# Window attention of a fused two-layer kernel: units of two images (128 query rows by 64 keys), the last four queries of each image in a path of their own

## What is computed

```python
# 16 heads of width 16, per image of S = 68 tokens
q, k, v = (x @ Wq + bq), (x @ Wk + bk), (x @ Wv + bv)      # split into 16 heads
scores = einsum('bhqd,bhkd->bhqk', q, k) / sqrt(16)
allowed = (j <= i) & (i - j < 64)                          # causal, a window of 64 keys
attn = softmax(where(allowed, scores, -1e30))
out = einsum('bhqk,bhkd->bhqd', attn, v) ... @ Wo + bo
```

## Time and profile before

| | |
|---|---|
| median of 3 runs | 1057.34 us (1054.91 to 1061.70) |
| the profiled execution: its time | 1059.86 us |
| the profiled execution: its span, first to last instruction | 1058.1 us |
| mean granted TensorE clock over the span | 0.965 |
| the attention stage, from its first to the first instruction of the next | 52.5 to 225.3 us, 172.8 us |
| TensorE busy in it | 170.6 us |
| DVE / ACT / POOL busy in it | 143.5 / 117.7 / 98.6 us |

### The profile page before, as it was taken

How to read it: one execution, slowest core, us unless ns; L and a number is a source line. 1 busy time by engine, 2 the same in 40 slices (tenths; PEclk the granted TensorE clock), 3 DMA queues, 4 the chain that set the end, 5 groups by cost and what they waited for, 6 DMA issues and landing times. The chain is left out here.

```text
span 1058.1 us, 29663 instructions
## 1 busy us (share of the span) xinstructions
PE 947.0 (90%) x10380; PEld 745.1 (70%) x10398; DVE 589.4 (56%) x1463; ACT 413.5 (39%) x1102; POOL 520.6 (49%) x714
## 2 busy tenths in 40 slices
PE   8899999988747999999999998789888957999996
PEld 6667777777634888888888876355556635888895
DVE  1778888865994777433333325676887551111111
ACT  2267677734243344444443422222333222333431
POOL 0055665610604777777777627777772002433432
PEclk9999999999969999999999999887999987999998
DMA  7010000002004888877788723344483056476650
GB/s 256 1 46 2 0 0 0 1 12 75 1 1 161 292 283 261 272 247 224 242 265 253 230 89 100 100 113 122 122 289 80 21 191 218 143 262 222 266 155 25
DMA packets 79820, 149.28 MB, mean 141 GB/s; under 512 B 18892, under 2 KB 53327, under 8 KB 75760
## 3 DMA queue, kind: packets, MB, share of 16 engines
q1 hardware_dynamic: 34768, 77.15, 21.7%
q0 software_dynamic: 17712, 47.88, 16.0%
q10 hardware_dynamic: 27248, 23.09, 6.5%
HBM read 200.22 MB, written 31.73 MB: 219 GB/s over the span
## 5 line engine op out<-in xcount | busy, mean ns | idle before, releaser
L1332 POOL DMA_INDIRECT x_x<-m_x_rows,x_idx x170 | 165.7, 975 | 75.1 <-issue 35.6
L1358 PE MATMUL x_pup<-x_xt,x_w 128*128 128x128 f32 (+1 forms) x2176 | 182.9, 250 | 0.0
L1358 PEld LDWEIGHTS x_pup<-x_xt,x_w 128*128 128x128 f32 (+1 forms) x2176 | 166.9, 165 | 5.9 <-issue 5.7
L1623 POOL DMA_INDIRECT rl_y<-m_y_rows,rl_idx x136 | 134.2, 986 | 43.6 <-issue 36.3
L1439 DVE TENSOR_TENSOR x_hid<-x_gate,x_pup 128x128 f32<-128x128 f32 x170 | 48.9, 288 | 148.3 <-ACT x_gate L1411 140.9
L1372 PE MATMUL x_pdown<-x_w,x_hid 128*128 128x256 f32 (+1 forms) x408 | 104.2, 389 | 0.3 <-DVE x_y L1446 0.3
L1407 ACT ACTIVATE x_xt<-x_pturn 128x256 f32<-128x256 f32 x170 | 65.3, 384 | 89.3 <-PE x_pturn L1343 86.2
L442 POOL TENSOR_TENSOR wa_probs<-wa_probs,wa_peak 68x544 f32<-68x544 f32 x64 | 69.9, 1092 | 57.6 <-DVE wa_peak L593 54.9
L2420 DVE TENSOR_TENSOR x_y<-x_pdown,x_b 128x256 f32<-128x256 f32 x21 | 8.9, 425 | 151.7 <-PE x_pdown L2374 151.7
L2406 ACT ACTIVATE x_hid<-x_pup,x_b 128x128 f32<-128x128 f32 (+1 forms) x200 | 52.8, 357 | 95.9 <-PE x_pup L2357 95.8
L1411 ACT ACTIVATE x_gate<-x_pup 128x128 f32<-128x128 f32 x170 | 47.2, 278 | 92.4 <-PE x_pup L1358 91.7
(11 more groups left out here) (344 smaller groups left out, 1904.7 us busy)
## 6 DMA issues: line engine op xcount, KB each, us to landing
x_w<-in_experts SPq DMA_DIRECT2D x204, 384.0 KB
late_w<-in_w SPq DMA_DIRECT2D x28, 1024.0 KB
m_y_rows<-x_y ACTq DMA_DIRECT2D x170, 128.0 KB
xT<-in_w SPq DMA_DIRECT2D x12, 1024.0 KB, 6.0
xn<-in_w SPq DMA_DIRECT2D x10, 1024.0 KB, 10.3
h<-in_w SPq DMA_DIRECT2D x10, 1024.0 KB, 14.0
m_x_rows<-xn SPq DMA_DIRECT2D x34, 128.0 KB, 1.8
x_x<-m_x_rows,x_idx POOLq DMA_INDIRECT x170
```

Of the source, the lines that this page charges most:

```text
L1332: nc.gpsimd.indirect_dma_start(x[:, s, :], None, x_rows, bass.IndirectOffsetOnAxis(ap=idx[:, s:s + 1], axis=0))\
L1358: mm = nc.tensor.matmul(pup[rows:rows + wide, bank, m * P + side * wide:m * P + (side + 1) * wide], w[:, lane, first:first + wide], xt[:, ...
L1623: nc.gpsimd.indirect_dma_start(y[:, t % YR, kk, :], None, y_rows, bass.IndirectOffsetOnAxis(ap=idx[:, n:n + 1], axis=0))\
```

## The change

A unit becomes two images by one half: the first 64 queries of both images are the 128 partitions, the first 64 keys of 8 heads the 512 columns. There are 32 units (16 pairs of images by two halves, c changing fastest), unit u = step; all is written out, with no loop. A block of 4 images is four steps. Row sums are now a reduction on DVE (`add_up`) of the exponentials, followed by a reciprocal of 8 columns per row, and POOL multiplies the probabilities by it (`normalise`) before they are transposed; the matmuls by ones are gone. Transposes take two heads at once (128x128, eight per unit). The values are stored for both images' 64 tokens with the two heads of a pair block-diagonal (`vals`, two heads times 64 keys = 128 rows by 32 columns), so a weighing is 16 matmuls of 128 rows, 32 output partitions and 64 columns.

The last four queries (which see 68 keys) go a way of their own, once per pair of images: 2 images x 16 heads x 4 queries = 128 rows by 68 keys. In it DVE has seven more kinds of instruction (`last_spread`, `last_mask`, `last_peak`, `last_shift`, `last_invert`, `last_normalise`, `last_pick`), TensorE four (scores, `last_turn`, `last_weigh`, `last_sum`) and ACT three (`last_exp`, `last_move`, `last_place`). The values of the last four tokens of four images are a job of their own (`vt`, `vtail`).

The core of the diff (constants, buffers, waits and the old bodies are left out; the old bodies stand above):

```diff
@@ tensor
+                def score(unit):
...
+                    for i in range(2):
                         for g in range(STRIPS):
                             strip = slice(g * STRIP, (g + 1) * STRIP)
+                            mm = nc.tensor.matmul(pscore[i * HALF:(i + 1) * HALF, g, 0:P], queries[strip, i, :],
+                                                  kheads[strip, unit % 2, i, :, :].rearrange("p m n -> p (m n)"),
                                                   start=True, stop=True)
+                    if c == 0:
...
+                        for i in range(2):
+                            for cc in range(DC):
...
+                                mm = nc.tensor.matmul(pl_score[at:at + LROWS, :],
+                                                      lq[:, pair % 2, cc, i, :, :].rearrange("p h q -> p (h q)"), keys[:, i, :],
+                                                      start=True, stop=True)
+                    mm.then_inc(scored, 1)
...
+                    for n in range(2):
+                        first = blk * CB + (2 * int(kind[1]) + n) * S
+                        for kc in range(DC):
+                            for odd in range(2):
+                                mm = nc.tensor.matmul(pjob[odd * HALF:(odd + 1) * HALF, n * P:(n + 1) * P],
+                                                      xT[:, kc, first:first + HALF], wv[:, kc, odd * P:(odd + 1) * P],
+                                                      start=(kc == 0), stop=(kc == DC - 1))
...
+                def last_turn(pair):
+                    pe.wait_ge(l_ready, pair + 1)
...
+                    nc.tensor.transpose(pl_main, lmain[:, :, :].rearrange("p o n -> p (o n)"), ident)
+                    nc.tensor.transpose(pl_tail, ltail[:, :, :].rearrange("p n q -> p (n q)"), ident).then_inc(l_turned, 1)
+
+                def last_weigh(pair):
+                    slot, first = pair // 2 % 2, pair % 2 * 2
+                    pe.wait_ge(l_moved, pair + 1)
+                    pe.wait_ge(jobs_moved, done_by(2 * pair, "vt"))
+                    for i in range(2):
+                        for c in range(DC):
+                            at = (i * DC + c) * LROWS
+                            nc.tensor.matmul(pl_out[at:at + LROWS, :], lmainT[:, at:at + LROWS],
+                                             vals[:, slot, first + i, c * (HC // 2):(c + 1) * (HC // 2), :]
+                                             .rearrange("p t n -> p (t n)"), start=True, stop=False)
+                            mm = nc.tensor.matmul(pl_out[at:at + LROWS, :], ltailT[:, at:at + LROWS],
+                                                  vtail[:, slot, c * P:(c + 1) * P], start=False, stop=True)
+                    mm.then_inc(l_weighted, 1)
+
+                def last_sum(pair):
+                    pe.wait_ge(l_picked, pair + 1)
+                    nc.tensor.matmul(pl_sum, lout[:, :, :].rearrange("p h n -> p (h n)"), const("row_sel"),
+                                     start=True, stop=True).then_inc(l_summed, 1)
+
+                pe.wait_ge(w_in, 96)
+                for (blk, kind), into in zip(FIRST, (pout, pjob, pturn, plast)):
+                    project(wq if kind[0] == "q" else wk, int(kind[1]), blk, into)
+                for step in range(STEPS + 3):
+                    jobs = jobs_of(step)
+                    if step < STEPS:
+                        score(step)
+                    if step >= 3:
+                        weigh(step - 3)
+                    if step >= 3 and step % 2 == 1:
+                        last_weigh((step - 3) // 2)
+                    for job in jobs[:1]:
+                        do_job(*job)
+                    if step >= STEPS:
+                        keep_running(3)
+                    if 0 <= step - 2 < STEPS:
+                        turn(step - 2)
+                    for job in jobs[1:]:
+                        do_job(*job)
+                    if 2 <= step < STEPS + 2 and step % 2 == 0:
+                        last_turn(step // 2 - 1)
+                    if step >= 3 and step % 2 == 1:
+                        last_sum((step - 3) // 2)
+                keep_running(3)
@@ gpsimd
+                nc.gpsimd.memset(vals[:, :, :, :, :], 0.0).then_inc(vals_set, 1)
...
+                spread(0)
+                for step in range(STEPS + 1):
+                    if step + 1 < STEPS:
+                        spread(step + 1)
+                    if step < STEPS:
+                        shift(step)
+                    if step >= 1:
+                        normalise(step - 1)
@@ vector
+                for step in range(STEPS + 3):
+                    even = step % 2 == 0
+                    if step < STEPS:
+                        mask(step)
+                        if even:
+                            last_mask(step // 2)
+                        find_peak(step)
+                        if even:
+                            last_peak(step // 2)
+                            last_shift(step // 2)
+                    if 1 <= step <= STEPS:
+                        add_up(step - 1)
+                        invert(step - 1)
+                    if even and 2 <= step <= STEPS:
+                        last_invert(step // 2 - 1)
+                        last_normalise(step // 2 - 1)
+                    if not even and (step + 1) // 2 < NPAIR:
+                        last_spread((step + 1) // 2)
+                    if not even and step >= 3:
+                        last_pick((step - 3) // 2)
@@ scalar
+                    if even and step >= 4:
+                        last_place((step - 4) // 2)
+                    if 0 <= step - 3 < STEPS:
+                        place(step - 3)
+                    if 1 <= step <= STEPS:
+                        exp(step - 1)
+                    if not even and step <= STEPS:
+                        last_exp((step - 1) // 2)
+                    for job in jobs[:1]:
+                        move_job(*job)
+                    if 0 <= step - 2 < STEPS:
+                        move_turned(step - 2)
+                    for job in jobs[1:]:
+                        move_job(*job)
+                    if even and 2 <= step < STEPS + 2:
+                        last_move(step // 2 - 1)
```

More of the change, by code:

```diff
@@ L529, in body @@
[L529 to L539 removed]
+                        nc.tensor.matmul(pjob[:, 0:D], wq[:, 0, 0:P], wq[:, 1, :], start=True, stop=True)
@@ L554, in body @@
-                        if not (start and step < 3):
-                            v = (step - 3) % UNITS
-                            weigh(unit - 3, (step - 3) % 2, v % ABLK, v // ABLK, start and step == 3)
-                blocks(pe, body)
-                n_units = NBLK * UNITS
-                for step in range(3):
-                    keep_running(pjob, 2)
-                    if step < 2:
-                        turn(n_units + step - 2, (step - 2) % 4, step % 2, False)
-                    v = (step - 3) % UNITS
-                    weigh(n_units + step - 3, (step - 3) % 2, v % ABLK, v // ABLK, False)
@@ new lines, in score, with turn @@
+                    mm.then_inc(scored, 1)
+                def turn(unit):
+                    pe.wait_ge(normalised, unit + 1)
+                    if unit:
+                        pe.wait_ge(turn_moved, unit)
+                    for two in range(HC // 2):
+                        mm = nc.tensor.transpose(pturn[:, two * P:(two + 1) * P],
+                                                 probs[:, unit % 4, 2 * two:2 * two + 2, :].rearrange("p h n -> p (h n)"), ident)
+                    mm.then_inc(turned, 1)
@@ new lines, in _ @@
+                act.wait_ge(w_in, 96)
+                for (blk, kind), src in zip(FIRST, (pout, pjob, pturn, plast)):
+                    move_job(blk, kind, src)
+                for step in range(STEPS + 4):
+                    even = step % 2 == 0
+                    jobs = jobs_of(step)
+                    if even and step >= 4:
[14 more added lines that the diff above has]
+                        last_move(step // 2 - 1)
```

486 lines of the change are left out of this document (256 added, 230 removed).

## The result

The changed kernel takes 1148.65 us (median of 3 runs, 1141.46 to 1152.25), against 1057.34 us before: ratio 1.0824, 95% interval 1.0769 to 1.088. It is 91 us slower. The forecast was 1069 and its range ended at 1083. The profiled execution took 1152.25 us.

A forecast was written before the change was run, and what follows sets the result against it. TensorE was taken to bound the attention stage. Its step terms summed to 16 W - 30.0, +11.6 us at W = 2.6, so 1057.3 + 11.6 = 1069 us; range 1034 to 1083, likeliest case 1056 to 1078.

The forecast's parts named there:

- The wait at `last_turn`: In even steps TensorE waits about 0.1 us for `l_ready` from DVE's chain, making the step 4.7 us.
- TensorE's list as the bound: The attention stage is as long as TensorE's work; DVE, ACT and POOL stay below TensorE's 4.5 us per step.
- The granted clock stays 1.00: In the attention stage the clock stays at 1.00, as TensorE stays busy.
- W: Time of one `last_weigh` on TensorE in odd steps: between 0.46 and 3.0 us, taken as 2.6; no change at 1.9.
- that the term of 0.90: Time of a unit's transposes on TensorE: 8 x 0.11, 0.90 us with what surrounds them.
- that of 0.65: Time of a unit's weighing on TensorE: 32 records in 0.61 us, 0.65 with one more change of array shape.
- 17.1 + 2 W: Length in us of a block of four steps in attention, against 20.3 for the same four images before.
- Cheap `last_weigh`: Rival: `last_weigh` takes 0.46 to 1.2 us, giving 1040 or 1035 us; chance 0.33 with or without the DVE hold.
- Halves in sequence: Rival: array halves do not overlap, scores 0.78 and value jobs 1.85 us, +20 on the forecast, 1089; chance 0.10.
- Fewer elementwise instructions, no time: Rival included in the forecast: DVE, ACT and POOL fall to about 100, 95 and 92 us without gain; no separate chance.
- DVE's chain sets steps: Rival: DVE holds steps at 3.4 us and `last_turn`'s wait at 4.5, gain ending near 1030; within cheap `last_weigh`'s 0.33.
- four signs of being wrong: `last_weigh` below 1.9 us, value jobs near 1.9, TensorE waiting for ACT's moves between jobs, or a stage outside attention moving.

The follow-up runs named there:

- e2: The changed kernel without the last four queries' path, their result columns filled by a copy of the input: 1004.81 us, ratio 0.9486.
- e5: The changed kernel with the last queries' spreading, shift, masking and normalising moved or folded so VectorE's work avoids GpSimd's way: 1058.74 us, ratio 1.0015.
- e8: The changed kernel with four unused matmuls run before `last_turn` in even steps, in place of TensorE's wait: 1099.07 us, ratio 1.0358.
- e4: The changed kernel with the last queries' later stages one step later and `last_weigh`'s 128-row matmuls grouped before its 16-row ones: 1078.22 us, ratio 1.0179.
- e3: The changed kernel with `last_turn`, `last_move`, `last_weigh`, `last_pick`, `last_sum` and `last_place` each one step later: 1083.85 us, ratio 1.0232.
- e7: The kernel before, with 16 unused groups of matmuls of `last_weigh`'s shapes and order added to its q/k jobs: 1106.76 us, ratio 1.043.
- e6: e5 with `last_weigh`'s four 128-row matmuls put first, then its four 16-row ones: 1033.69 us, ratio 0.9742.
- e11: The kernel before, with one unused 68x68 VectorE multiplication reading PSUM added ahead of each reciprocal: 1057.49 us.
- e9: e6 with `last_turn` and `last_sum` moved ahead of the step's second job: 1032.46 us, ratio 0.9731.

## Why the prediction was wrong

**The wait at `last_turn`, and with it TensorE's list as the bound: wrong.** The step that failed is the sentence that DVE's chain in an even step is "some 4.4 in all", so that `last_turn` "waits about 0.1". The chain from the mask to `l_ready` measured 145.53 - 140.49 = 5.04 us, where the forecast's own terms from the mask on (4.4 less 0.91 before it) make 3.5. TensorE came to `last_turn` 143.70 - 139.37 = 4.33 us after the step's scores, which is the 4.29 of the forecast (by chance: its terms were too long and part of the step ran at half clock). The small instructions were priced "0.15 to 0.33 each", from rows of other kinds: the earlier trace rows has a reciprocal, and a multiplication that reads PSUM and so keeps its 0.23 us under GpSimd's work. L669, L682 and L685 measured 1.01, 1.08 and 0.55. An estimate: with 0.34 for L685, as the two times that GpSimd was idle, and some 0.2 for the others, as L573's free 0.18 suggests, the chain would be about 1.9 us shorter, and the wait in that block was 1.89. The kernel before could not show the effect in attention, since its small DVE instructions there read PSUM; the prediction had no term for what GpSimd's work does to a small DVE instruction, and this change has them meet: L669 starts 0.09 us behind the shift on GpSimd every time (16 of 16).

**The granted clock stays 1.00: wrong, and the largest term.** "as TensorE stays busy" hung on the wait of 0.1. With waits of 2.25 us the clock was at 1.2 GHz for about half of the stage (its mean is 0.74). The sizes, by stage lengths: without the last queries 119.7 (e2); with them, the thin group at full clock and no long wait, 168.7 (e5), +49.0, of which 16 x 2.64 = 42; the changed kernel 255.9, +87.2 more. Of these, e8 takes back 48.5 by work alone, so at least that much was the clock. The other 38.7, by which e8's stage (207.4) is longer than e5's with the clock up in both, is left for the time that TensorE loses to DVE's chain, whether it is filled or not; that is an estimate, since the two kernels differ in more than this. What brings the clock down besides the long wait stays open (e4).

**W: right at 2.4 GHz, wrong as it ran.** Taken at 2.6 with bounds 0.46 to 3.0; measured 2.64 (e3) and 2.65 (e7) at full clock, 4.50 at half. The reasoning held too: putting equal shapes together brought 1.16 at half clock, and e6's stage is 26.9 us shorter by it, so 1.7 us of each 2.64 were changes of shape. The prediction's count by the Trainium skill, "TensorEngine Tiling (Array Packing)", Tiling Modes, that a change of mode drains TensorE, agrees with the trace (0.33 us for two records in turn, 0.34 for eight of one height), and the changes were avoidable.

**The count of transposes and of the weighing: wrong.** The prediction, and the section on the change ahead of it, put eight transposes and 16 weighing matmuls in a unit; both are errors. `turn` and `weigh` loop over `HC // 2` = 4, so it is four transposes (x4 records) and eight matmuls (x16 records). At full clock (e5, 130 to 150 us) the term of 0.90 measured 0.44 to 0.58, and that of 0.65 mostly 0.25 (0.22 to 0.36). The scores, put at 0.60, measured 0.40: the halves overlap fully. Together these terms were about 1 us per step too high, more than 30 us. The value job measured 1.03 (0.95), the q/k job 1.02, `last_sum` 0.22, first mask 57.68 (57.9).

**What that does to the sum.** With its own mechanism but right counts, the prediction would have been about 32 us lower, 1037, on the faster side; e5, which has that mechanism and no long wait, gave no change (1058.74 beside 1060.2). What stands between the two is seen in part only: e5's TensorE waits 5.9 us for jobs to be moved, which "just fit" in the forecast, the value jobs cost 0.08 more each, and the first three steps are slow (3.52, 6.96 and 4.42 us from mask to mask). A block of four steps is 19.42 us in e5, where the forecast's 17.1 + 2 W less 4 is 18.3. The rest of it stays open.

**The rivals.** Cheap `last_weigh`: the mechanism exists (e6), but not in this order. Halves in sequence: no. "Fewer elementwise instructions, no time": ACT and GpSimd fell as forecast, to 94.8 and 91.8, DVE did not: 139.6 instead of about 100, and that was the sign in the trace of what went wrong. DVE's chain sets steps: the nearest, but it was forecast as a smaller gain, since the price of TensorE standing still was left out. No rival had the clock in it. The 40% for slower came from W (0.31) and from halves in sequence (0.09), so that the direction came out was luck: it was given for other reasons than the true one. Of its four signs of being wrong one came, TensorE waiting for ACT's moves between two jobs, but small (3.7 us); the two that mattered, the wait at `last_turn` and the clock, were not among them.

## What to carry to other kernels

Price a small VectorE instruction by where its operands lie and by what GpSimd does at that moment: with everything in SBUF it can last as long as GpSimd's instruction (reductions and reciprocals kept their time here), while one that reads PSUM kept its time (e11), and work can be folded into ScalarE's exponential (e5). A wait of TensorE is not priced by its own length alone: check the granted clock behind it, and put matmuls into it, even useless ones (e8). Useful ones were tried on short waits only (e9), with a gain within the scatter. Group matmuls by shape within a stage and read how often a loop runs before pricing it (`HC // 2` was taken for `HC`).

## What the runs showed of the hardware

Waits of about 2 us each, one in some 15 us, cost at least 48.5 us through the clock (e8 against the changed kernel). After such a wait the granted clock was at 0.50 for some 10 us (130 to 140) though TensorE was busy throughout, while in e7 the same thin matmuls with no wait ahead left it at 0.99, and in e4 five waits of up to 1.9 us within 56 us left it at 1.00. Useless work made a kernel 50 us faster. A VectorE instruction on 68 or 16 columns in SBUF took 1.0 to 1.1 us under a GpSimd instruction of 1.04 us, while reductions and reciprocals in SBUF, and all that read PSUM, kept their time. And two matmuls of 16 and 128 rows in turn cost 0.33 us for each pair of records where, grouped, eight records take 0.34 (e6, 128 rows).
